# A Mamba layer and a gated feed-forward layer on one core: rings of the scan cut differently, and four turns of x moved behind the next z group

## The reference, cut to what matters

```
x = x + mamba(layernorm(x));  x = x + ffn(layernorm(x))

mamba: xn = layernorm(x) * gamma + beta
       x_ssm, z = split(xn @ W_in.T)                  # 1024 + 1024 channels
       x_ssm = silu(conv1d(x_ssm, 4 taps) + conv_b)
       xp = x_ssm @ W_xproj.T                         # 33 rows; B = 1..16, C = 17..32
       dt = softplus(xp @ W_dt.T + b_dt) + 0.001
       A = -exp(A_log)                                # 1024 channels x 16 states
       h_t = clip(exp(A dt_t) h_{t-1} + (1 - exp(A dt_t)) / (A + 1e-8) * B_t * x_t, -10, 10)
       y_t = sum_n C_t[n] h_t[n] + D x_t
       y = (y * silu(z)) @ W_out.T
ffn:   softmax gate, the top two of 7 weights normalized; shared + expert product + bias
```

## Time and profile before

| | us |
|---|---|
| median of 3 runs (lowest, highest) | 4684.94 (4679.14, 4690.98) |
| the profiled execution | 4684.51 |
| its span | 4682.7 |
| busy: PE, DVE | 4279.3 (91%), 3716.3 (79%) |
| busy: POOL, ACT | 3285.3 (70%), 3178.3 (68%) |
| POOL's multiply (line 953): busy, idle before it | 2379.6, 205.7 |
| DVE's recurrence (line 1091): busy, idle before it | 2408.9, 157.2 |

### The profile page before, as it was taken

One profiled execution on the slowest core, in us unless ns is written; L12 is line 12 of the kernel. 1 busy time (PEld: TensorE's weight loads), 2 busy tenths in 40 slices (PEclk: granted clock), 3 DMA queues, 4 the chain that ended last, 5 costly groups with the idle time before them and its releaser, 6 DMA issues. The chain is left out here.

```text
span 4682.7 us, 48765 instructions
## 1 busy us (share of the span) xinstructions
PE 4279.3 (91%) x14186; PEld 2517.8 (54%) x14186; DVE 3716.3 (79%) x4288; ACT 3178.3 (68%) x5820; POOL 3285.3 (70%) x1676
## 2 busy tenths in 40 slices
PE   2999999995999999999999999999999759999999
PEld 1777777773444444444444444444444337777777
DVE  5888888884999999999999999999999744444443
ACT  1655666654999999999999999999999611211111
POOL 0233323222889999999999999999999757777772
PEclk9999999997999999999999999999999879999999
DMA  5565556665566556656655665566556444545550
GB/s 182 188 201 184 199 184 195 195 201 183 150 185 172 155 161 185 169 156 167 187 161 149 174 187 160 151 182 188 159 152 184 135 150 153 161 154 164 168 158 31
DMA packets 591700, 786.65 MB, mean 168 GB/s; under 512 B 129712, under 2 KB 332848, under 8 KB 573512
## 3 DMA queue, kind: packets, MB, share of 16 engines
q1 hardware_dynamic: 580872, 762.56, 54.6%
q10 hardware_dynamic: 10560, 20.97, 1.2%
HBM read 540.17 MB, written 245.18 MB: 168 GB/s over the span
## 5 line engine op out<-in xcount | busy, mean ns | idle before, releaser
L1091 DVE TENSOR_TENSOR_SCAN g<-dd,carry,ps_a 128x512 f32<-128x512 f32 x2048 | 2408.9, 1272 | 157.2 <-ACT dd L964 122.9
L953 POOL TENSOR_TENSOR q<-g,cc 128x1024 f32<-128x1024 f32 x1024 | 2379.6, 2385 | 205.7 <-DMA cc<-c_d 125.1
L1031 PE MATMUL ps_y<-q,w_s 128*128 128x512 f32 x4096 | 2210.5, 622 | 128.0 <-POOL q L953 127.3
L1020 PE MATMUL ps_d<-dm,xk 99*128 99x512 f32 x2048 | 1570.1, 768 | 49.0 <-DMA dm<-band_d 39.8
L975 ACT ACTIVATE ps_a<-dt_s,small 128x512 f32<-128x512 f32 x2048 | 1475.7, 721 | 5.4 <-DVE g L1091 5.4
L964 ACT ACTIVATE dd<-ps_d 128x512 f32<-128x512 f32 x2048 | 1265.9, 619 | 197.4 <-PE ps_d L1020 185.2
L1031 PEld LDWEIGHTS ps_y<-q,w_s 128*128 128x128 f32 x4096 | 719.8, 193 | 847.1 <-POOL q L953 503.4
L1020 PEld LDWEIGHTS ps_d<-dm,xk 99*128 99x128 f32 x2048 | 393.7, 193 | 653.8 <-issue 412.9
L517 PE MATMUL ps_r_f<-xnt_hi,w_hi 128*128 128x512 f32 x1024 | 431.8, 422 | 13.8 <-DVE w_lo L683 13.8
L354 POOL TENSOR_TENSOR xnt_lo<-xnt_f,xnt_hi 128x512 fp32r<-128x512 f32 x64 | 85.2, 1331 | 478.8 <-ACT xnt_hi L392 478.8
L517 PE MATMUL ps_r_f<-xnt_lo,w_hi 128*128 128x512 f32 x1024 | 410.1, 400 | 0.0
(11 more groups left out here) (160 smaller groups left out, 4407.5 us busy)
## 6 DMA issues: line engine op xcount, KB each, us to landing
w_s<-w_d SPq DMA_DIRECT2D x128, 1024.0 KB, 5.2
xk<-xt_d SPq DMA_DIRECT2D x768, 132.0 KB
xt_d<-xt_f SPq DMA_DIRECT2D x256, 256.0 KB, 3.1
cc<-c_d SPq DMA_DIRECT2D x128, 512.0 KB, 11.5
dm<-band_d SPq DMA_DIRECT2D x192, 264.0 KB
xs_d<-xs_f SPq DMA_DIRECT2D x128, 256.0 KB, 2.7
zs_d<-zs_f SPq DMA_DIRECT2D x128, 256.0 KB, 2.6
dt_d<-lg_f SPq DMA_DIRECT2D x32, 1024.0 KB, 4.4
```

What stands on the lines that cost most here:

```text
L953: pool.tensor_tensor(q[:, s % QB:s % QB + 2, :], g[:, s % GB:s % GB + 2, :], cc[:, n:n + 2, :], ALU.mult).then_inc(s_q, 2)
L1020: pe.matmul(ps_d[:, i % 2, :], xk[:, (2 * blk + i // HALF) % XB, i % HALF, :], dm[:, i, :, :].rearrange("p t n -> p (t n)"), start=True, s ...
L1031: pe.matmul(ps_y[:, blk % 2, :], w[:, blk % 2, n * P:(n + 1) * P], q[:, s % QB, :], start=(n == 0), stop=(n == NS - 1)).then_inc(s_n, 1)
L1091: dve.tensor_tensor_scan(g[:, s % GB, :], dd[:, m % 2, n, :], ps_a[:, s % AB, :], carry[:, m, n:n + 1], ALU.add, ALU.mult).then_inc(s_g, 1)
```

## The change

It touches the scan's loads and the order of the first stage.

- `cc` becomes a ring of 10 pairs (20 rows). A pair's slot is its running number modulo 10, so a load waits for the pair ten before it. Pairs 0 and 1 of the next chunk are loaded in blocks 3 and 4, pairs 2 to 7 in the last block.
- `w_s` becomes a ring of 3 half blocks, each loaded by itself. The second half waits for `s_n` at half a block.
- `xk` becomes a ring of 3 half blocks instead of 4.
- The B numbers that `b_ahead` needs are gathered once for each sequence into a new HBM array `ba_d`; SP waits for both gathers, and each chunk's `b_ahead` reads 16 neighbouring numbers.
- In the first stage z group 0 comes before the first turn, each of the first four turns one z group later, on PE, ACT and SP; on DVE the lower parts of turns 0 and 1 come one convolution later. Three semaphores are merged into others (`s_wd`, `s_wdl`, `s_wdo` into `s_hi`, `s_lo`, `s_wt`).

The diff, cut to its core:

```diff
     # front, SP
-                    for m in range(4):
-                        store_zs(ch, m)
+                    store_zs(ch, 0)
+                    for m in range(4):
                         store_xs(ch, m + 4)
+                        store_zs(ch, m + 1)
                         store_turned(ch, m)
-                    store_zs(ch, 4)
     # front, ACT
+                    silu_z(ch, 0)
                     for m in range(4):
-                        silu_z(ch, m)
-                        if m < 3:
-                            silu_x(ch, 4 + m)
-                            upper_turned(ch, m)
-                        else:
-                            upper_turned(ch, m)
-                            silu_x(ch, 4 + m)
+                        silu_x(ch, 4 + m)
+                        silu_z(ch, m + 1)
+                        upper_turned(ch, m)
                         if m >= 2:
                             scale_xnt(ch + 1, m - 2)
-                    silu_z(ch, 4)
     # front, PE
+                    project(ch, "z", 0)
                     for m in range(4):
-                        project(ch, "z", m)
+                        project(ch, "z", m + 1)
                         turn_xs(ch, m)
...
-                    project(ch, "z", 4)
                     project_rows(ch, 6)
     # front, DVE
                     convolve(ch, 5)
-                    lower_turned(ch, 0)
                     convolve(ch, 6)
+                    lower_turned(ch, 0)
+                    convolve(ch, 7)
                     lower_turned(ch, 1)
-                    convolve(ch, 7)
                     lower_turned(ch, 2)
     # scan
-    XB, DTB, CN = 4, 3, 2
+    XB, DTB, CN, WB, CR = 3, 3, 2, 3, 10
-        w = sb("w_s", [P, 2, NS * P], c=c)
+        w = sb("w_s", [P, WB, NS * P // 2], c=c)
-        cc = sb("cc", [P, NS, CH], c=c)
+        cc = sb("cc", [P, CN * CR, CH], c=c)
     # scan, SP
-                def load_w(blk):
+                def load_w(blk, h):
                     if blk < BLOCKS:
-                        sp.dma_start(w[:, blk % 2, :], ...
+                        slot = (2 * blk + h) % WB
+                        sp.dma_start(w[:, slot, :], w_d[blk % MD, :, bass.ds(W_DIAG + NS * P // 2 * h, NS * P // 2)])
                 def load_c(ch, i):
                     if ch < CHUNKS:
-                        if ch > 0:
-                            sp.wait_ge(s_q, multiplied(STEPS * ch - NS + CN * (i + 1)))
+                        pair = ch * (NS // CN) + i
+                        slot, old = pair % CR, pair - CR
+                        if old >= 0:
+                            sp.wait_ge(s_q, multiplied(STEPS * (old // (NS // CN) + 1) - NS + CN * (old % (NS // CN) + 1)))
                 def load_ahead(ch):
-                    row = xp_d[b, 1:1 + NS, bass.ds(k * CH, 1)].rearrange("n o -> (n o)")
-                    sp.dma_start(b_ahead[:, :], row.partition_broadcast(P),
+                    sp.dma_start(b_ahead[:, :], ba_d[ch // NCH, ch % NCH, :].partition_broadcast(P))
+                def gather_ahead(b):
+                    sp.dma_start(ba_d[b, :, :], xp_d[b, 1:1 + NS, 0:LEN].rearrange("n (k t) -> k n t", t=CH)[:, :, 0],
...
                 load_x(1, 0)
+                sp.wait_ge(s_dps, HALF)
                 load_x(1, 1)
-                load_w(0)
+                load_w(0, 0)
+                load_w(0, 1)
                 load_c(0, 2)
                 load_c(0, 3)
+                for b in range(BATCH):
+                    gather_ahead(b)
+                sp.wait_ge(s_ba, 16 * BATCH)
                 load_ahead(0)
                 load_prev(0)
-                sp.wait_ge(s_dps, HALF)
-                load_x(2, 0)
                 for blk in range(BLOCKS):
                     sp.wait_ge(s_dps, made)
-                    load_x(blk + 2, 1)
+                    load_x(blk + 2, 0)
...
-                        for i in range(4 if ch == 0 else 6, 8):
+                        for i in range(4 if ch == 0 else 8, 8):
                             load_c(ch, i)
...
+                    if m in (3, 4):
+                        load_c(ch + 1, m - 3)
                     if m == MD - 1:
-                        load_c(ch + 1, 0)
+                        load_c(ch + 1, 2)
                     if blk > 0:
                         sp.wait_ge(s_n, NS * blk)
-                    load_w(blk + 1)
+                    load_w(blk + 1, 0)
...
                     if m == MD - 1:
-                        load_c(ch + 1, 1)
-                        load_c(ch + 1, 2)
+                        load_c(ch + 1, 3)
+                        load_c(ch + 1, 4)
...
-                    load_x(blk + 3, 0)
+                    load_x(blk + 2, 1)
                     if m == MD - 1 and more:
-                        load_c(ch + 1, 3)
+                        load_c(ch + 1, 5)
                         load_ahead(ch + 1)
                     if blk > 0:
                         store_y(blk - 1)
...
                     if m == MD - 1:
-                        load_c(ch + 1, 4)
-                        load_c(ch + 1, 5)
+                        load_c(ch + 1, 6)
+                        load_c(ch + 1, 7)
+                    if blk + 1 < BLOCKS:
+                        sp.wait_ge(s_n, NS * blk + NS // 2)
+                    load_w(blk + 1, 1)
```

More of the change, by code:

```diff
@@ L62, in build @@
         y_d = nc.dram_tensor("y_d", [BATCH, MD, P, LEN], F32).ap()
+        ba_d = nc.dram_tensor("ba_d", [BATCH, NCH, NS], F32).ap()
         ident = sb("ident", [P, P])
@@ L73, in build @@
             front(nc, sb, sem, t_in, ident, ones, minus_half, margin, within, clips, xs_d, dt_d, zs_d, xp_d, xt_d, bt_d, c_d)
-        scan(nc, sb, sem, ident, clips, xs_d, dt_d, xp_d, xt_d, bt_d, band_d, c_d, w_d, y_d)
+        scan(nc, sb, sem, ident, clips, xs_d, dt_d, xp_d, xt_d, bt_d, band_d, c_d, w_d, y_d, ba_d)
         ffn(nc, sb, sem, t_in, ident, minus_half, xs_d, zs_d, xp_d, w_d, y_d, out)
@@ L302, in _ @@
                     sp.dma_start(dst, src).then_inc(s_wt, 16)
-                sp.wait_ge(s_wdl, 1)
-                sp.dma_start(w_dt[2 * NX:NX3, :].bitcast(F32), low_dt.bitcast(F32)).then_inc(s_wdo, 16)
+                sp.wait_ge(s_lo, 3)
+                sp.dma_start(w_dt[2 * NX:NX3, :].bitcast(F32), low_dt.bitcast(F32)).then_inc(s_wt, 16)
                 load_x(1)
@@ L445, in _ @@
                                    stage[:, :, :].rearrange("p m t -> p (m t)"), ACT.Copy).then_inc(s_hi, 1)
-                act.activation(w_dt[:, :], raw_dt, ACT.Copy).then_inc(s_wd, 1)
+                act.activation(w_dt[:, :], raw_dt, ACT.Copy).then_inc(s_hi, 1)
                 for ch in range(CHUNKS):
@@ L458, in _ @@
                     else:
-                        act.wait_ge(s_wdl, 1)
+                        act.wait_ge(s_lo, 3)
                     keep_z(ch, 3)
@@ L581, in _ @@
                     if ch == 0:
-                        pe.wait_ge(s_wdo, 16)
+                        pe.wait_ge(s_wt, 14 * 16)
                     for i in range(SUB):
@@ L747, in _, with scan @@
                 dve.wait_ge(s_fl, 3)
-def scan(nc, sb, sem, ident, clips, xs_d, dt_d, xp_d, xt_d, bt_d, band_d, c_d, w_d, y_d):
+def scan(nc, sb, sem, ident, clips, xs_d, dt_d, xp_d, xt_d, bt_d, band_d, c_d, w_d, y_d, ba_d):
     STEPS = MD * NS
@@ L785, in scan @@
         s_dm = [S(f"dm{i}") for i in range(PIECES)]
-        s_xk, s_cc = [S(f"xk{i}") for i in range(XB)], [S(f"cc{i}") for i in range(NS // CN)]
+        s_xk, s_cc = [S(f"xk{i}") for i in range(XB)], [S(f"cc{i}") for i in range(CR)]
         s_dtl = [S(f"dt{i}") for i in range(DTB)]
-        s_wl, s_xp, s_yo = ([S(f"{n}{e}") for e in range(2)] for n in ("w", "xp", "yo"))
+        s_xp, s_yo = ([S(f"{n}{e}") for e in range(2)] for n in ("xp", "yo"))
+        s_wl = [S(f"w{i}") for i in range(WB)]
         s_dps, s_dd = S("dps"), S("dd")
@@ L939, in _ @@
                     sp.wait_ge(s_xp[e], 16 * BLOCKS // 2)
-                sp.wait_ge(s_ba, 16 * CHUNKS)
+                sp.wait_ge(s_ba, 16 * (BATCH + CHUNKS))
             @block.gpsimd
@@ L947, in _ @@
                     ch, n = s // STEPS, s % NS
+                    pair = ch * (NS // CN) + n // CN
                     if s % STEPS < NS:
-                        pool.wait_ge(s_cc[n // CN], ch * 16 + 16)
+                        pool.wait_ge(s_cc[pair % CR], 16 * (pair // CR) + 16)
+                    rows = cc[:, CN * (pair % CR):CN * (pair % CR) + CN, :]
                     pool.wait_ge(s_g, s + 2)
@@ L952, in _ @@
                         pool.wait_ge(s_n, s - QB + 2)
-                    pool.tensor_tensor(q[:, s % QB:s % QB + 2, :], g[:, s % GB:s % GB + 2, :], cc[:, n:n + 2, :],
+                    pool.tensor_tensor(q[:, s % QB:s % QB + 2, :], g[:, s % GB:s % GB + 2, :], rows,
                                        ALU.mult).then_inc(s_q, 2)
@@ L1028, in sum_state @@
                             pe.wait_ge(s_fin, blk - 1)
```

(6 more changed lines are left out.)

20 lines of the change are left out of this document (10 added, 10 removed).

## The result

The changed kernel took 4547.85, 4548.45 and 4551.6 us in three runs, a median of 4548.45; the kernel before took 4685.11 beside it (median of four). The ratio is 0.971, with an interval of 0.9691 to 0.9729: 2.9% faster. The forecast was 4548.

The account below looks back on a forecast made before the run. The prediction took the scan as paced by DVE, with 132 us idle, mostly at chunk boundaries where C rows come late behind b_ahead in a full queue. 4684.5 - 127 - 4 - 6 = 4547.5, say 4548; range 4515 to 4610.

Parts of the forecast that it names:

- The boundaries: Scan, 15 chunk boundaries: the 132 us DVE idles there go, less 5 us for small waits; gain 127 us.
- some 5 us forward: Scan boundary: contiguous b_ahead alone would bring the issue of the fifth pair of C rows some 5 us forward.
- The slack of 5 us: Scan boundary: the second x half lands at 2125 and is wanted at 2130.1, the smallest slack, 5 us.
- the sum of the queue from 2089 on: Scan boundary: bytes queued, counted at 225 GB/s, give landing times for x halves and pair 7; none is late.
- T = 0: Scan: the start of the last block of a chunk on DVE, put at 2101.9 in the kernel before.
- The allowance of 5 us for small waits: Scan: unknown small waits bounded by 0 and 10 us in all, taken as 5, 0.3 us a boundary.
- The start: Start of the scan: gathers land near 1175, C rows are issued near 1179, 4 us earlier; gain 4 us.
- my outer bound, a loss of 1.5: Start of the scan: if the gather lands as late as b_ahead did, C leaves at about 1184.5, losing 1.5 us.
- The first stage: First stage: PE's 3.05 us wait at the first turn becomes one on DVE; 0.4 us a chunk, gain 6 us.
- the rival that won all 46 us: First stage: DVE's lower half is never in the way, all 46 us are won, 4508 us; chance 0.08.
- an x ring that stops PE in every block: Scan: three x halves land too late, PE stops every block, slower than before, 4802 us at 2 us each; chance 0.03.
- a chunk set by DVE: First stage: DVE's chain sets the chunk, a loss of 1 us each, 4570 us; chance 0.05.

Follow-up runs that it names:

- e1_gather: The kernel before, with b_ahead alone read from a gathered array and nothing else of the change: 4614.87 us, ratio 0.984.
- e2_ring: The changed kernel, with b_ahead read as before (2048 single elements a chunk, no gather): 4654.52 us, ratio 0.9929 to the kernel before.
- e5_start: The changed kernel, with the gathers issued earlier, behind the first half of x: 4545.6 us, ratio 0.9707 to the kernel before.
- e3_front: The kernel before, with the changed kernel's first stage and nothing else: 4678.1 us, median of ten runs, ratio 0.9979.
- e4_turn: The changed kernel, with DVE's lower halves of turns 0 and 1 again ahead of conv groups 6 and 7: 4513.83 us, ratio 0.963.

## Why the prediction was right

The time came out within 2 us of the forecast, which is less than the runs of one kernel differ among themselves (4547.85 to 4551.6), so that much nearness is luck. The two profiled executions are 132.9 us apart, where the parts forecast add up to 137. The boundaries, which make nearly all of it, came as forecast; one small term had the wrong sign, and another was right in size for a reason only half foreseen.

- **The boundaries: 127 forecast, 129.6 measured.** The chain was as I read it: hole and full queue make the fifth pair of C late, SP's order and the ring put it ahead, the gather closes the hole. I gave the two parts no separate numbers except "some 5 us forward" for the gather; e1_gather has 4.9 us a boundary for it alone (8.8 - 3.9). The two don't simply add up: gather alone 74 us, the changed rings and order alone 22 (e2_ring), together 129.6. Each leaves something late that the other cures.
- **The slack of 5 us was not there.** I said I would be wrong if PE waits for xk or w_s in the scan, and it does, 8.3 and 11.0 us in all, at the boundaries. The failed step is the sum of the queue from 2089 on. It starts with an empty queue and counts bytes at 225 GB/s. By it the second x half lands 23.1 us behind T = 0 and is wanted at 28.2; at the boundary shown, where T = 0 is 2205.1 (32 steps of 1.172 us before 2242.63, the end of DVE's long run), it landed at 27.1 (2232.20) and PE wanted it at 26.4. And the sum has no deadline for the second half of w, which is issued at 2226.39, lands at 2240.8 and was wanted 1.5 us earlier. The outcome held since PE's lead over DVE covers waits of 0.2 to 2 us. The allowance of 5 us for small waits took this in (2.4 measured), so the number was right for a reason only half named. e2_ring shows what the same transfer costs when it is 6 us later: 7 us a boundary.
- **The start: 4 won forecast, 3.1 lost.** This term was mis-sized, and its sign was wrong; my outer bound, a loss of 1.5, did not hold it either. The step that failed is the time of the gathers. I took them to land some 9 us behind 1166 and C to leave at 1179, 12.3 us behind the place where b_ahead was issued. This row of the kernel before has that place:

```profile
1166.72 0.74 SPq L854 DMA_DIRECT2D b_ahead<-xp_d  x1
```

  From there to the C pairs it was 16.4 us before (to 1183.09), and in the changed kernel it is 16.4 us from the gathers' issue to the C pairs (1163.37 to 1179.73), 13.3 of them until SP goes on. So the gathers won nothing over what they replaced. That 1176.7 and 1179.7 stand close to my 1175 and 1179 is chance, since mine were counted in the kernel before, whose scan begins later. The second part is that the full queue gives only half of the first stage's gain on: the scan's first transfer moved 6.8 us forward (1132.09 to 1125.29), DVE's first step 6.0, but the gathers only 3.4 against b_ahead's old place, 2.7 us less than DVE's step. e1_gather, which has the first stage and the rings of before, shows the loss without this second part. SP's timeline of e1_gather:

```profile
1168.34 1.39 SPq L857 DMA_DIRECT2D ba_d<-xp_d  x2
1183.04 0.35 SPq L853 DMA_DIRECT2D b_ahead<-ba_d  x1
...
1187.79 2.52 SPq L848 DMA_DIRECT2D cc<-c_d  x4
```

  The gathers hold SP until 14.7 us behind their issue, and from them to the C pairs it is 19.5 us. C leaves 4.7 us later than before (1.6 of it are there already at the gathers), and the way from the first step to step 16 is 4.7 us longer (34.2 in place of 29.5). The Trainium skill (DMA: Bandwidth & Descriptors, Specifications) has transfers under 512 B done as read-modify-write, and by it I had put the gain at 2 in place of 4, still with the wrong sign. Its anatomy of one DMA, which the prediction sets beside it, is that of a transfer issued by GpSimd, and SP issues these. The wait was indeed longer than the 9 us I had from rows. The trace bears out no more than that 256 single elements behind 2 MB of w and C held SP for 11.9 us; what of that is queue and what the small writes' own time, no run here separates. Issued early, they go with a first DVE step 5.5 us later (e5_start).
- **The first stage: 6 forecast, 6.0 in the profile, 10 by e3_front's ten runs.** The trade of one wait for another came as worked out: 2.3 us on turn 2 forecast, 2.24 measured, and 0.36 left of the 3.05 at the first turn. The composition was not foreseen. I had one length for all chunks and no clock in the sum. Like against like, the trade won 0.11 us in a chunk with a fall of the clock and 0.26 in one without, in place of 0.4; the mean came to 0.4 because the clock fell 8 times in place of 10. Why it falls less often behind the shorter stop stays open. e4_turn shows what turn 2's wait still held back: without it the chunk is 60.8 us, 3.0 below before, and DVE's first scan step comes 42 us earlier than before (1123.1 against 1165.3). So the rival that won all 46 us is nearly what the z order alone gives, but by another sum than the one I made: some 16 of the 42 are the ten falls of the clock (10 x 1.6), not the stops themselves.
- The rivals of an x ring that stops PE in every block, and of a chunk set by DVE, did not come: between boundaries DVE runs unbroken, and chunks got shorter.

## What to carry to other kernels

A full transfer queue is one shared delay: in this kernel the load issued with the least time before its use seemed to be the bottleneck, and curing that one alone (e2_ring) handed the wait to the next. Find what blocks the queue itself, here 8 KB in 2048 pieces, and cure that together with the order. When one stage is made to end earlier, set each later transfer against the new demand, not the old one: behind a full queue only half of the gain was passed on here. And when work is moved ahead on one engine, look at what the partner engine's order then puts in its way, which here was worth more (37 us) than the move itself brought (6 us in the profile).

## What was not expected of the hardware

- TensorE's granted clock fell to the lower of its two levels behind a single stop of 2.24 us in a stage where PE is busy 90% of the time: 1.00 up to the stop, 0.65 in the 3.6 us behind it, 0.85 in the next 3. Behind the stop of 3.05 us before the change it was the same in 10 of 14 chunks: this is a chunk of the kernel before, with PE's stop up to 566.20.

```profile
564.00:566.00 2.00, 0.00 (x0) 0.00 (x0) 2.00 (x5) 0.97 (x2) 0.31 (x1) 1.00 0.00 0
566.00:568.00 2.00, 1.80 (x8) 1.50 (x9) 1.93 (x5) 0.64 (x2) 0.00 (x0) 0.71 0.51 182
568.00:570.00 2.00, 2.00 (x7) 1.51 (x6) 1.89 (x6) 0.18 (x1) 0.00 (x0) 0.50 1.02 383
570.00:572.00 2.00, 2.00 (x11) 1.52 (x10) 1.93 (x3) 1.53 (x3) 0.00 (x0) 0.94 0.94 348
```

  In the chunk at 503 that the prediction rests on, a stop of the same length had no such fall (1.00 from 503 to 511). The price is 64.1 - 62.4 = 1.7 us a chunk where it falls (1.6 before the change), about as much as taking the stop away brings (62.4 - 60.8). Why it falls behind one stop and not behind the next of the same length stays open. The Trainium skill (TensorE: Matmul & The Clock Gate, Part 1) describes a throttle that idle time sets and activity releases, and the rows agree in that. It also has the monitor run freely, not in step with the kernel, which would fit equal stops with and without a fall; no run here shows it.
- A load of 8 KB in 2048 pieces cost the scan 4.9 us of idle a boundary with the old rings (before against e1_gather) and 7.2 with the new (e2_ring against the changed kernel), though its bytes are under 0.1% of the 9.9 MB queued there.
